# The floor's fraction in the last feed-forward block: from VectorE to ScalarE and GpSimd

## The reference

```
h = float2fix(einsum('bsd,df->bsf', x, w1) + b1, 8)      # multiples of 1/256
xq = float2fix(h, 8)
y = interp(xq, linspace(-4, 4, 33), gelu at those points)  # 0 below -4, identity above 4
h = float2fix(y, 8)
out = float2fix(einsum('bsf,fd->bsd', h, w2) + b2, 8)
x = layernorm(x + out)
```

## Time and profile before

| | |
|---|---|
| median of 3 runs | 2759.33 us |
| lowest, highest | 2757.91, 2769.3 us |
| the profiled execution | 2757.93 us, span 2756.1 us |
| the stage's own work, first `up` to last output sum | 2577.15 to 2724.96 us, 147.8 us |
| its layer norm, up to the last instruction on `xT` | to 2748.5 us |
| mean granted TensorE clock | 0.878 |

### The profile page before, as it was taken

One profiled execution on the slowest core, in us unless ns is written; L12 is line 12 of the kernel. 1 busy time (PEld: TensorE's weight loads), 2 busy tenths in 40 slices (PEclk: granted clock), 3 DMA queues, 4 the chain that ended last, 5 costly groups with the idle time before them and its releaser, 6 DMA issues. The chain is left out here.

```text
span 2756.1 us, 37344 instructions
## 1 busy us (share of the span) xinstructions
PE 2108.4 (76%) x13171; PEld 1389.4 (50%) x13177; DVE 1655.9 (60%) x4425; ACT 959.2 (35%) x1790; POOL 853.9 (31%) x807
## 2 busy tenths in 40 slices
PE   6987679886887864876689675878778787678786
PEld 3544369744544442652354334666666666535332
DVE  2753411176654677436574766677887877536686
ACT  0242324310440421222034472344444444334343
POOL 1001132250000037441000005777777777203000
PEclk9999679998998967997899896889989898879998
DMA  9200157347008153643500107222222222130000
GB/s 236 78 21 3 60 195 263 118 98 193 20 22 214 34 214 139 224 127 136 109 17 20 76 0 191 71 60 63 59 55 64 58 68 61 36 90 1 0 0 31
DMA packets 135561, 242.90 MB, mean 88 GB/s; under 512 B 42336, under 2 KB 80352, under 8 KB 128872
## 3 DMA queue, kind: packets, MB, share of 16 engines
q1 hardware_dynamic: 70335, 128.79, 16.2%
q0 software_dynamic: 56416, 102.76, 12.6%
q10 hardware_dynamic: 8640, 9.19, 1.2%
HBM read 267.52 MB, written 70.25 MB: 123 GB/s over the span
## 5 line engine op out<-in xcount | busy, mean ns | idle before, releaser
L3014 POOL DMA_INDIRECT L2f_G<-in_L2f_table,L2f_idx x512 | 533.7, 1042 | 174.7 <-issue 153.0
L3365 DVE CUSTOM_DVE_ANT_0 L2f_junk<-L2f_G,L2f_X 128x256 bf16<-128x256 f32 x512 | 182.6, 421 | 133.4 <-DMA L2f_G<-in_L2f_table,L2f_idx 133.2
L3089 PE MATMUL psum<-L2f_G,L2f_diag 128*128 128x256 f32 x768 | 185.4, 393 | 0.0
L3089 PEld LDWEIGHTS psum<-L2f_G,L2f_diag 128*128 128x128 f32 x768 | 150.0, 198 | 33.1 <-issue 9.5
L3066 PE MATMUL psum<-xT,L2f_mw 128*128 128x256 f32 x512 | 136.0, 414 | 9.1 <-DVE L2f_h L3371 9.0
L1192 PE MATMUL psum<-constb 128*128 128x256 bf16 x512 | 92.0, 283 | 62.9 <-PEq L994 39.1
L3229 ACT ACTIVATE L2f_diag<-const,L2f_actd 128x128 f32<-128x128 f32 x400 | 123.9, 388 | 29.5 <-DVE L2f_actd L3379 29.5
L2364 POOL DMA_INDIRECT picks_x<-L1f_rows,L1f_put x64 | 71.0, 1110 | 190.9 <-DVE L1f_sm L2577 171.7
L3066 PEld LDWEIGHTS psum<-xT,L2f_mw 128*128 128x128 f32 x512 | 107.4, 212 | 29.5 <-DVE L2f_h L3371 11.1
L3222 ACT ACTIVATE L2f_actd<-L2f_dots 128x9 f32<-128x9 f32 (+1 forms) x64 | 13.4, 210 | 282.7 <-DVE L2f_dots L3365 282.7
L3076 PE MATMUL psum<-L2f_h,L2f_mw 128*128 128x256 f32 x256 | 73.7, 414 | 44.4 <-DVE L2f_acc L3415 44.4
(11 more groups left out here) (667 smaller groups left out, 4961.9 us busy)
## 6 DMA issues: line engine op xcount, KB each, us to landing
L1f_we<-in_L1f_w SPq DMA_DIRECT2D x32, 384.0 KB, 9.5
picks_x<-zeros SPq DMA_DIRECT2D x16, 544.0 KB, 8.9
L1f_xe<-picks_x SPq DMA_DIRECT2D x32, 272.0 KB, 3.0
picks_y<-zeros SPq DMA_DIRECT2D x16, 512.0 KB, 6.5
L2f_G<-in_L2f_table,L2f_idx POOLq DMA_INDIRECT x512, 2.8
slots_x<-zeros POOLq DMA_DIRECT2D x8, 512.0 KB, 8.0
L1f_wb<-in_L2x_w SPq DMA_DIRECT2D x1, 4096.0 KB, 12.1
L1f_g<-picks_y SPq DMA_DIRECT2D x8, 512.0 KB, 12.2
```

What stands on the lines that cost most here:

```text
L3014: nc.gpsimd.indirect_dma_start(out=G[:, h, k, :], out_offset=None, in_=ins["L2f_table"], in_offset=bass.IndirectOffsetOnAxis(ap=IDX[:, t, ...
L3089: mm = nc.tensor.matmul(ps[:, MIX + t % 2, 0:D], diag[:, i % 2, k, :], row[:, D:2 * D], start=(h == 0 and k == 0), stop=(h == HEADS - 1 an ...
L3365: e = VE.tensor_tensor_reduce(out=junk[:, k, :], in0=row[:, 0:D], in1=X[:, t % 3, :], scale=1.0, scalar=0.0, op0=ALU.mult, op1=ALU.add, ac ...
```

## The change

ScalarE gets one more instruction for each unit, ahead of its two GELUs: `plain` = `u4` - `ROUND4`, the floor without its offset, as an Identity with a bias. GpSimd gets 16 subtractions `fr` = `plain` - `xq`. VectorE's L1936, and its wait for `floored`, are gone. There are two new signals. `floor_plain` tells GpSimd that `plain` is written. `above` tells VectorE that `fr` is there (`second` waits for it behind its first instruction), and it holds back the next writer of `plain` (ScalarE) and of `xq` (VectorE) of the same buffer. There is one more tile of two buffers, `plain`.

```
             @block.gpsimd
+                for u in range(NU):
+                    pool.wait_ge(s["floor_plain"].sem, s["floor_plain"].at(u + 1))
+                    if u >= 2:
+                        pool.wait_ge(s["hidden"].sem, s["hidden"].at(u - 1))
+                    nc.gpsimd.tensor_tensor(fr[:, u % 2, :], plain[:, u % 2, :], xq[:, u % 2, :], ALU.subtract).then_inc(s["above"].sem, 1)
...
                 def ends(u):
                     if u >= 2:
                         act.wait_ge(s["hidden"].sem, s["hidden"].at(u - 1))
+                        act.wait_ge(s["above"].sem, s["above"].at(u - 1))
+                    nc.scalar.activation(plain[:, k, :], u4[:, k, :], ACT.Identity, bias=shift[:, 0:1]).then_inc(s["floor_plain"].sem, 1)
...
                 def first(u):
+                    if u >= 2:
+                        dve.wait_ge(s["above"].sem, s["above"].at(u - 1))
...
-                    dve.wait_ge(s["floored"].sem, s["floored"].at(u + 1))
-                    link(nc.vector.scalar_tensor_tensor(fr[:, k, :], u4[:, k, :], -ROUND4, xq[:, k, :], ALU.add, ALU.subtract))
...
                 def second(u):
                     link(nc.vector.tensor_tensor(g1[:, k, :], g1[:, k, :], g0[:, k, :], ALU.subtract))
+                    dve.wait_ge(s["above"].sem, s["above"].at(u + 1))
```

More of the change, by code:

```diff
@@ L112 @@
            "pk_down", "pk_dots", "pk_gate", "pk_mix", "pk_diag", "pk_used", "pk_ycopy", "pk_yturn", "pk_yadd", "pk_dadd",
-           "padded_v", "q_clear", "k_clear", "laid_q", "laid_k", "put0", "put1", *(f"laid_a{n}" for n in range(4)), "sc_done", "mx_done", "mt_done", "mt_copied", "st_done", "ex_done", "av_done", "av_free",
+           "padded_v", "q_clear", "k_clear", "floor_plain", "above", "laid_q", "laid_k", "put0", "put1", *(f"laid_a{n}" for n in range(4)), "sc_done", "mx_done", "mt_done", "mt_copied", "st_done", "ex_done", "av_done", "av_free",
            "at_done"]
@@ L1835, in sb @@
             return ctx.enter_context(nc.sbuf_tensor(f"{name}_{nm}", shape, dt))
-        y, xq, u4, fr, g0, g1, h = (sb(k, [P, 2, 2 * CH]) for k in ("y", "xq", "u", "fr", "g0", "g1", "h"))
+        y, xq, u4, fr, g0, g1, h, plain = (sb(k, [P, 2, 2 * CH]) for k in ("y", "xq", "u", "fr", "g0", "g1", "h", "plain"))
         acc = sb("acc", [P, DH, T])
@@ L1962, in _ @@
                 s["dve_chain"].base += link.n
-        for k in ("ends", "rounded", "hidden_pe", "hidden", "floored", "down_pe"):
+        for k in ("ends", "rounded", "hidden_pe", "hidden", "floored", "down_pe", "floor_plain", "above"):
             s[k].base += NU
```

## The result

| | before | changed |
|---|---|---|
| median, 22 executions each | 2761.79 us | 2769.14 us |
| ratio of the changed kernel to the one before | | 1.0031, 95% interval 1.0021 to 1.0041 |
| the profiled execution, its span | 2757.93, 2756.1 us | 2779.51, 2777.7 us |
| the stage, first `xq` to the end of the last output sum | 140.84 us | 151.51 us |
| the same in a second profile | 140.79 us | 151.56 us |

The changed kernel is slower by 0.31%: 7.4 us between the medians, 5.8 to 11.3 us by the interval. Single executions of either kernel spread over 18 to 24 us, but that is not in this stage: in two profiles of each its own time repeats to 0.05 us. The profiled execution of the changed kernel is a long one, 21.6 us above the one before; 11.0 of them lie ahead of the stage (the first `xq` starts at 2595.12 against 2584.12) and 10.7 in it.

The account below looks back on a forecast made before the run. Bound: VectorE and TensorE waiting for each other in turn in the last stage. Ring 7.1, output steps 3.7 and start 1.0 make 11.8 us, added to the profiled 2757.93: 2769.7 us, range 2761 to 2779.

Parts of the forecast that it names:

- the exclusion: Last stage: GpSimd's subtraction, taken as 2.31 us, and VectorE's SBUF instructions block each other; the later one waits.
- the late GELUs: ScalarE: `plain` ahead of the GELUs delays them past VectorE's need; L1942 could start 0.38 us later than before.
- the ring: VectorE and TensorE wait for each other in turn; each pair of units 0.95 us longer, 7.5 pairs, 7.1 us.
- the output steps: Three VectorE output steps inside the stage, less covered by spare time: 1.2 us each, 3.7 us in all.
- The start: Start of the stage: `plain` stands before the table load and first GELUs, on which VectorE already waited: 1.0 us.
- nothing is excluded: Rival, chance 0.19: GpSimd and VectorE run side by side, only late GELUs count: 4 us, 2762 to 2764 us.
- The clock falls in every pair: Rival, chance 0.25: longer TensorE waits lower its clock, some five more pairs pay 1.7 us: 8.5 us more, 2778.
- VectorE's gain comes through: Rival, chance 0.05: GELUs not late, each pair falls by 1.26 us: 9.5 us off, 2748.5 us.

Follow-up runs that it names:

- with the ring open: TensorE runs three `up` ahead instead of two; in the kernel before, this alone gave a stage of 129.53 us against 140.84.
- the first experiment: The changed kernel with GpSimd subtracting only 128 of 1024 columns and VectorE's multiplication reading `xq` instead of the fraction: stage 148.50 us.
- the short subtraction with the ring open: The changed kernel with three `up` ahead, GpSimd subtracting 128 of 1024 columns, VectorE's multiplication reading `xq`: stage 120.59 us.

## Why the prediction was right, and where it was off

The forecast of 2769.7 us met a median of 2769.14. That it met it to 0.6 us is luck: the forecast started from one execution, 2757.93, the median before was 2761.79, and the medians lie 7.4 us apart, not 11.8. The stage's own time is the fairer test, 10.7 us against 11.8, and the mechanism holds: the exclusion and the late GELUs make the loss. But the sum came so near because its errors cancel: the ring was taken 1.6 us too long and the output steps 3.5, and two holds of 2.0 us each had no term. Term by term:

- **The ring.** 0.95 us a pair; measured 0.79 (16.51 - 15.72), in pairs without an output step. The places are those of the prediction: VectorE waits for g1, L1948 is held up to GpSimd's end and ends 1.08 us behind it, the lower of my two values, and GpSimd's own work is 2.3 to 2.4 us. Over seven pairs that is 5.5 us, against 7.1: the last unit has no `first` behind it and pays nothing (6.36 us between the last two `h` before, 6.37 after), and I had counted it as half a pair.
- **The output steps.** 3.7 us; measured 0.2. From `h` to `h` the pair with the first step takes 17.63 us against 16.18 before, 0.7 more than a pair's 0.79 accounts for, since VectorE had 0.65 to 0.78 us to spare in a pair and not the 0.2 that I had worked out. The second step shares its pair with a `down` at the lower clock (2688.84) and vanishes behind it: 18.03 us are the 16.50 of a pair and the 1.5 of that `down`, where before the step took 0.46 us. The third stands between the last two `h`, behind the last `first`, and costs nothing.
- **The end.** No term; measured 2.0 us. Behind unit 14 ScalarE has no bank left to empty, so `plain` of unit 15 follows at once, and the subtraction of unit 15 falls on L1950 of unit 14. The 5.5, the 0.2 and these 2.0 make the 7.7 us between first and last `h`.
- **The start.** 1.0 us; measured 3.0 (13.70 us from the first `xq` to the first `h`, against 10.71). The 1.0 us ahead of the GELUs is there, the other 2.0 is a hold that I had not looked for: GpSimd's second subtraction, of unit 1, falls on L1951 of unit 0, which takes 3.26 us at 2605.53. This term was mis-sized by a factor of three.

The two holds that had no term, with GpSimd's rows beside them:

```profile
2605.53 3.26 DVE L1951 TENSOR_TENSOR L3f_fr<-L3f_fr,L3f_g 128x1024 f32<-128x1024 f32 x1
...
2727.97 3.26 DVE L1950 SCALAR_TENSOR_TENSOR L3f_fr<-L3f_fr,L3f_g 128x1024 f32<-128x1024 f32 x1
```

```profile
2605.24 2.46 POOL L1857 TENSOR_TENSOR L3f_fr<-L3f_plain,L3f_xq 128x1024 f32<-128x1024 f32 x1 [3.14 <-ACT L3f_plain L1912]
...
2727.34 2.81 POOL L1857 TENSOR_TENSOR L3f_fr<-L3f_plain,L3f_xq 128x1024 f32<-128x1024 f32 x1 [0.48 <-ACT L3f_plain L1912]
```

- **Exclusion.** Shown by runs: the subtraction alone costs 6.2 us, 9.8 with the ring open, an eighth of it lets the gain through, and a memset in its place costs nothing between first and last `h`. That the fast kind is held too, which the trace of before did not show, is in the rows of 2.73 us.
- **The late GELUs.** Shown by the run with ScalarE's instruction alone: 4.6 us. The prediction's 0.38 us a pair is what the pair of 16.11 us in the first experiment shows; seven of them are 2.7 us, the start is 1.0, and the first `down` ran at the lower clock for 1.1 us longer (6.52 us against 5.39). Together 4.8, which is 0.2 over; the steps and the other `down` were not taken apart.

The rivals: *nothing is excluded* would have given 4 us and up to 2 for the clock; the kernel nearest to it gave 7.7, since six `down` ran at the lower clock. So even that case was further from zero than I had it. *The clock falls in every pair* did not come true, but my reason for that was wrong. The wait did stay split between both units in several pairs (1.63 and 0.74 us at 2644.42 and 2652.29), yet the place of the turn does not hold: I had put the turn between a wait of 1.7 and one of 1.95 us, and `down` behind waits of 2.49 and 2.55 us took 3.70 us while those behind 2.50 and 2.60 took 5.17 and 5.40. That their number stayed at four I had assumed, not worked out; what sets it stays open. *VectorE's gain comes through* is what the short subtraction with the ring open shows, and only there.

## What to carry to other kernels

Before work is moved from VectorE to GpSimd, look whether both would read SBUF at the same time: then most of GpSimd's time comes on top of VectorE's, 2.0 of 2.36 us here for an instruction of 1.26 us saved, and the move can pay only where VectorE stands idle at just that moment, or where that sum comes out the other way. Look at the first and last units too: there the subtraction fell on other instructions than in the middle, for 4 of the 10.7 us. An instruction that is put ahead of a result in its engine's queue is late by its own length there; see first how early the result is (0.68 us here, against 1.04). And where two engines wait for each other in turn, look first at the order in which they walk: one more `up` ahead took 11.3 us off this stage, more than the 8.9 that dropping VectorE's instruction could give behind it.

## What the runs showed of the hardware

- GpSimd's `tensor_tensor` on two SBUF tiles and a VectorE instruction with SBUF inputs exclude each other: the one that starts second waits for the end of the first, in either direction, also VectorE's fast kind (0.69 us became 2.73). The later one then ends 1.08 us behind the other's end instead of the 1.23 that it takes alone, 0.55 in place of 0.69. In steady work with the ring open VectorE's held instruction took 3.26 us in place of 1.23, beside a subtraction of 2.36 us.
- A GpSimd memset of 2560 columns (2.23 us) held none of the VectorE instructions with two SBUF inputs beside it (means of 1225 and 1226 ns), and it was not held by them; the one of the fast kind that started beside it took 0.83 us in place of 0.69.
- GpSimd's time in the profile has its wait in it: 2.36 us unheld, 3.16 us on average with the ring open, where nearly every one had to wait (most of them 3.34 or 3.35 us). Its busy time of 50.5 us in the open ring is not 50.5 us of work.
- The length of TensorE's wait alone does not say what clock follows: behind 2.49 and 2.55 us of it `down` took 3.70 us, behind 2.50 and 2.60 us 5.17 and 5.40, and behind 1.95 us in the kernel before 5.40, each at the same place in the second profile of its kernel; with three `up` ahead `down` took 3.70 behind 1.95 us. Such a loss was mostly 1.4 to 1.7 us, at most 3.1 (6.76 us at the end of the run with the memset).
- The stage's own time repeats to 0.05 us while whole executions spread over 18 to 24 us, so that single profiles could tell differences of half a microsecond here. The exception is the clock: one `down` more or less at the lower clock, or a longer one, moves a stage by 1.4 us or more.
